# The mixture's first token group computed at the end of the scan's program, and the groups taken in the order 0, 2, 1, 3

## The chip, the core and the metric

The kernel runs on one NeuronCore of a Trainium2 chip. TensorE (PE in the profile, PEld for its weight loads), VectorE (DVE), ScalarE (ACT), GpSimd (POOL) and the sync engine (SP, which here only issues DMAs) each take their own list of instructions in order; semaphores order them against each other. The metric is the device time of one execution in microseconds (us), lower is better.

## What is computed

Two layers on x of shape 2 x 1024 x 256 in float32. Layer 0 is a causal linear attention and a feed-forward net with 2:4 sparsity. Layer 1 is a test-time-training scan and a mixture of experts; the change touches only these last two:

```python
x = x + ga * scan(layernorm(x) * (1 + ca) + sa)       # 64 minibatch steps of 16 tokens,
                                                      # out = layernorm(z) * gamma + beta, then @ Wo.T
h = layernorm(x) * (1 + cb) + sb
logits = h @ gate_w                                   # 8 experts, the best 2 by softmax
h1 = gelu(einsum('nd,edh->neh', h, w1) + b1)          # 8 experts of width 128
routed = einsum('ne,ned->nd', gates, einsum('neh,ehd->ned', h1, w2) + b2)
shared = gelu(h @ shared_w1 + shared_b1) @ shared_w2 + shared_b2
x = x + gb * (routed + shared)
```

## The kernel before, in words

Tokens lie in 16 tiles of 128 (x_sb): tiles 0 to 7 are batch row 0, tiles 8 to 15 batch row 1. The program has one block of instruction lists for each phase; a block ends with a barrier of all engines. The change touches the blocks of the last two phases.

**The scan** (scan_phase) walks eight chunks c; a chunk holds tile c of both batch rows and eight steps n. A step is values (L1628), residual on VectorE (L1428, u_done), gradient (L1640) and new_w on VectorE (L1433); other work, written out by hand, lies beside each step. The outputs z of a chunk go through DRAM or, for the last chunk, by small DMAs (L1223) to tokens on partitions; keep_z (L1270, GpSimd) makes z from them. Then follow, a chunk or two later, z_norm and z_aggregate (VectorE), z_rstd_of (GpSimd, L1275 and L1277), z_centre (VectorE, L1448), out_turn (TensorE, L1589), drain_out (ScalarE, L1363), the projection out_rows (TensorE, L1615), the gate out_rows (VectorE, L1455) and add_rows (GpSimd, L1290, x_done). In chunk 7 the normalised tiles 0 to 3 are turned (turn_group, L1730), drained (drain_group_norm, L1741), and split into a high part (L1413, hi_done) and a low part (GpSimd, L1330, hl_done): they are the mixture's group 0.

**The scan's tail**, after the last step, still has chunk 6's drain_out and out_rows and the whole chain of chunk 7. TensorE's list there is keep_warm(8), out_rows of chunk 6, out_turn(7), keep_warm(2), out_rows of chunk 7. keep_warm (L1659) multiplies the identity with a weight and nobody reads the result.

**The mixture** (moe_phase) takes four groups of four tiles, software-pipelined: the loop's turn g computes group g's outputs (shared_rows, expert_rows, weigh) beside group g+1's inner blocks. The first turn, g = -1, has only the latter: ten hidden(0, m) of six matmuls each (L1966), logits (L1949, sixteen matmuls), the turn of group 1 (L1730) and gates_turn (L1956). On ScalarE it has ten gelu activations (L1841) with bias, on VectorE memsets of gates (L1922), norms of group 1 (L204, L207), gating (L1868 to L1898), centring (L220) and split_group (L1749, L1751), on GpSimd two constants (L1807, L1808), an inverse root (L213) and ratio_of (L1813), which gating waits for in its middle. hidden(n) waits for the gelu two before it, since the PSUM tensor hid has two halves. The turn g = 0 begins with hidden(1, 0).

## Time and profile of the kernel before

| | us |
|---|---|
| median of three runs | 1066.62 |
| the three runs | 1066.62, 1066.68, 1062.79 |
| the profiled execution, its own time | 1061.99 |
| the profiled execution, its span | 1060.0 |

| engine | busy us | share of the span |
|---|---|---|
| PE | 995.6 | 94% |
| PEld | 800.8 | 76% |
| DVE | 678.6 | 64% |
| ACT | 332.5 | 31% |
| POOL | 250.2 | 24% |

The profile shows one execution. Durations are of one instruction or of a run of like instructions; PE's ends are modelled, so that for a series of matmuls the distance from one start to the next is the safer measure. "PE busy" counts every matmul, read or unread. The granted clock of TensorE is 0.986 of full speed in the mean; 1.00 is 2.4 GHz, 0.50 is 1.2 GHz.

### The profile page before, as it was taken

Reading aid. Unit: us, or ns where it says so; the run is one execution under the profiler, and the core shown is the slowest. Engines: PE = TensorE matmul, PEld = TensorE weight load, DVE = VectorE, ACT = ScalarE, POOL = GpSimd, SP = SyncE. Lnnn points to the kernel's source line nnn. Section 1 sums busy time; section 2 is a strip of 40 time slices with the busy share of each in tenths; the row PEclk is TensorE's granted clock in tenths of the full one; section 3 lists DMA queues with packets and bytes.
Section 4 is the critical chain, followed back from the end, with each engine's and each line's share of the span. In section 5 each row is a group of like instructions: output and inputs, shape, how many; then the busy total and the mean of one; then the engine's idle time right before and its main releaser. Section 6 shows DMA issues by size and latency. Waiting matters only on the chain. (4 is left out here: it accounts for less than half of the span.)

```text
span 1060.0 us, 15726 instructions
## 1 busy us (share of the span) xinstructions
PE 995.6 (94%) x6016; PEld 800.8 (76%) x6016; DVE 678.6 (64%) x1494; ACT 332.5 (31%) x604; POOL 250.2 (24%) x319
## 2 busy tenths in 40 slices
PE   6899999999999999999779999977999997999997
PEld 4688888888888888888668888864666664887875
DVE  6766676666676666666648887562667763466556
ACT  4343333343433333433224232102132421422220
POOL 2222222222221222222010100123344633111011
PEclk9999999999999999999999999998999999999999
DMA  9300000000000000000030000002544430000000
GB/s 293 134 2 1 1 1 1 1 1 2 1 1 1 1 1 1 2 1 1 20 124 10 1 1 1 1 1 44 139 128 97 87 72 7 1 16 16 11 21 20
DMA packets 33051, 33.37 MB, mean 31 GB/s; under 512 B 6857, under 2 KB 26834, under 8 KB 32978
## 3 DMA queue, kind: packets, MB, share of 16 engines
q1 hardware_dynamic: 32978, 32.38, 11.0%
q8 instruction: 48, 0.79, 0.3%
q14 instruction: 25, 0.20, 0.1%
HBM read 23.98 MB, written 8.13 MB: 30 GB/s over the span
## 5 line engine op out<-in xcount | busy, mean ns | idle before, releaser
L393 POOL TENSOR_TENSOR rope_sum<-rope_cos,rope_sin 128x512 f32<-128x512 f32 x80 | 114.9, 1436 | 257.2 <-DVE rope_sin L514 257.2
L429 ACT ACTIVATE rope_exp<-rope_sum 128x512 f32<-128x512 f32 x80 | 50.5, 631 | 205.5 <-POOL rope_sum L393 205.4
L783 PE MATMUL proj<-wo_sb,attn_out_t 128*128 128x256 f32 x512 | 113.2, 379 | 0.7 <-issue 0.7
L783 PEld LDWEIGHTS proj<-wo_sb,attn_out_t 128*128 128x128 f32 x512 | 96.1, 190 | 13.4 <-issue 0.9
L732 PE MATMUL num<-v_ones,score_masked 128*128 128x129 f32 x512 | 100.2, 278 | 5.9 <-DVE score_masked L572 5.9
L733 PE MATMUL num<-state,q_t 128*128 128x129 f32 x512 | 99.9, 277 | 0.0
L1910 DVE SCALAR_TENSOR_TENSOR m_acc<-m_expert,gates,m_acc 128x256 f32<-128x256 f32 x128 | 61.9, 484 | 49.0 <-PE m_expert L1991 42.2
L732 PEld LDWEIGHTS num<-v_ones,score_masked 128*128 128x128 f32 x512 | 83.0, 193 | 13.4 <-DVE score_masked L572 8.0
L511 DVE TENSOR_TENSOR rope_cos<-proj,cos_sb 128x512 f32<-128x512 f32 x80 | 55.3, 691 | 52.5 <-PE proj L686 52.5
L686 PE MATMUL proj<-w_hi,a_h_hi 128*128 128x512 f32 x192 | 79.4, 494 | 4.0 <-DVE w_lo L136 2.1
L733 PEld LDWEIGHTS num<-state,q_t 128*128 128x128 f32 x512 | 78.6, 194 | 0.0
L526 DVE SCALAR_TENSOR_TENSOR feat<-rope_sum,rope_exp 128x512 f32<-128x512 f32 x80 | 69.1, 864 | 6.9 <-ACT rope_exp L431 6.9
L724 PE MATMUL score<-q_t,k_t 128*128 128x512 f32 x128 | 66.9, 605 | 0.0
L1991 PE MATMUL m_expert<-w_sb,m_act 128*128 128x256 f32 x256 | 62.9, 385 | 3.3 <-DVE m_acc L1910 3.3
L1072 PE MATMUL f_rows<-wd_sb,hidden 128*128 128x256 f32 x256 | 58.1, 380 | 5.4 <-DVE f_dx L991 2.9
L1433 DVE TENSOR_TENSOR t_w<-g_ps,head_blocks 128x512 f32<-128x512 f32 x64 | 44.3, 691 | 29.0 <-PE g_ps L1640 28.9
L714 PEld LDWEIGHTS turn<-ident,feat 128*128 128x128 f32 x320 | 38.1, 142 | 32.3 <-issue 25.8
L686 PE MATMUL proj<-w_lo,a_h_hi 128*128 128x512 f32 x192 | 61.1, 399 | 0.0
L686 PE MATMUL proj<-w_hi,a_h_lo 128*128 128x512 f32 x192 | 61.0, 399 | 0.0
L1072 PEld LDWEIGHTS f_rows<-wd_sb,hidden 128*128 128x128 f32 x256 | 48.2, 190 | 13.9 <-issue 6.0
L1991 PEld LDWEIGHTS m_expert<-w_sb,m_act 128*128 128x128 f32 x256 | 47.3, 190 | 14.9 <-DVE m_acc L1910 8.8
L714 PE MATMUL turn<-ident,feat 128*128 128x128 f32 x320 | 46.4, 276 | 9.8 <-ACT k_t L416 9.8
(218 smaller groups left out, 1905.3 us busy)
## 6 DMA issues: line engine op xcount, KB each, us to landing
kv_scratch<-t_kv SPq DMA_DIRECT2D x16, 256.0 KB, 2.5
kv_rows<-kv_scratch SPq DMA_DIRECT2D x32, 128.0 KB, 3.5
a_stage<-in_wqkv SPq DMA_DIRECT2D x6, 512.0 KB, 5.5
wo_sb<-in_wo SPq DMA_DIRECT2D x1, 2048.0 KB, 9.4
a_stage<-in_wgu SPq DMA_DIRECT2D x4, 512.0 KB, 9.6
out<-x_sb SPq DMA_DIRECT2D x16, 128.0 KB, 1.7
u_scratch<-u_rows SPq DMA_DIRECT2D x28, 64.0 KB, 2.8
t_u<-u_scratch SPq DMA_DIRECT2D x14, 128.0 KB, 2.1
```

What stands on the lines that cost most here:

```text
L393: pool.tensor_tensor(y[:, parity], t1[:, parity], t2[:, parity], ALU.add).then_inc(s["y_done"], 1)
L511: dve.tensor_tensor(t1[:, parity].rearrange("p (g d) -> p g d", d=HD // 2), proj[:, bank, :].rearrange("p (g d) -> p g d", d=HD // 2), cc. ...
L526: dve.scalar_tensor_tensor(dst, y[:, parity], 0.0, ex[:, parity], ALU.max, ALU.add).then_inc(s["feat_done"], 1)
L686: mm = pe.matmul(proj[:, bank, :], hh[:, parity, k, :], ww[:, k, cols], start=(i == 0 and k == 0), stop=(i == 2 and k == KD - 1))
L714: t = pe.transpose(turn[:, bank(j), r * P:(r + 1) * P], src[:, r * P:(r + 1) * P], ident[:])
L724: pe.matmul(score[:, g % 2, :], k_t[:, g, :], q_t[:, g, :], start=True, stop=True).then_inc(s["score_full"], 1)
L732: pe.matmul(dst, am[:, g % 2, r * P:(r + 1) * P], v[:, b, g, :], start=True, stop=False)
L733: mm = pe.matmul(dst, q_t[:, g, r * P:(r + 1) * P], state[:, b, g, :], start=False, stop=True)
L783: mm = pe.matmul(proj[:, b, 0:D], o_t[:, i, :], wo[:, i, :], start=(i == 0), stop=(i == H - 1))
L1072: mm = pe.matmul(rows[:, n % 2, 0:D], hid[:, g % 2, m, i * P:(i + 1) * P], wd[:, m, :], start=(m == 0), stop=(m == NM - 1))
L1910: ins = dve.scalar_tensor_tensor(acc[:, n % 2], expert[:, k % 2, j * D:(j + 1) * D], gates[:, g % 2, i, e:e + 1], acc[:, n % 2], ALU.mult, ...
L1991: mm = pe.matmul(expert[:, k % 2, j * D:(j + 1) * D], act_t[:, g % 2, e, toks], w2[:, e, :], start=True, stop=True)
```

## The change

The mixture's turn g = -1 is taken out of moe_phase. Its instructions now stand in the scan's block, behind the last step, between those of chunks 6 and 7, and keep_warm(8) and keep_warm(2) are gone. The helpers gating, gates_turned, logits, gates_turn, ratio_of and hidden become methods with the same instructions; ScalarE's hidden is now called gelu. The PSUM tensors of the scan are used for them: kv_ps for hid, z_ps for small, g_ps for turn. The other part is the order of the groups: tiles 0 to 3, 8 to 11, 4 to 7, 12 to 15, so that the second group's tiles are those of chunks 0 to 3 of batch row 1. The memsets of gates go to the start of VectorE's list in the scan, GpSimd's constants to the end of its chunk 0, and the low part of group 0 moves forward in GpSimd's chunk 7, from its end to just before z_rstd_of. The three staging slots of the mixture's weights now lie in the tensor that the first group's gelu outputs are written to. In GpSimd's tail, z_rstd_of(7) now stands before add_rows(6).

The diff, cut to its core:

```diff
+TURNS = (0, 2, 1, 3)
...
-    def group_norm(self, s):
+    def group_norm(self, s, order=tuple(range(NG))):
...
-                dve.bn_stats(stats[:, i, :], x[:, g * GT + i, :]).then_inc(s["stat_done"], 1)
+                dve.bn_stats(stats[:, i, :], x[:, order[g] * GT + i, :]).then_inc(s["stat_done"], 1)
...
+        self.e_act = [self.keep.enter_context(nc.sbuf_tensor("m_act0", [P, NH, GT * P], F32))]
...
-            self.stage_for(ctx, "t_stage", NCH, 3)
+            self.first, self.slots = NCH, 3
+            self.stage = self.e_act[0][:].rearrange("p m t -> p (m t)")[:, 0:3 * KD * WCH].rearrange(
+                "p (s k n) -> p s k n", s=3, k=KD)
...
-            _, e_rstd, _ = self.group_norm(e_s)
+            e_norms, e_rstd, e_centre_group = self.group_norm(e_s, TURNS)
...
+                    if not nxt:
+                        pool.wait_ge(e_s["hi_done"], 1)
+                        pool.tensor_tensor(self.e_h_lo[:, 0], self.e_h[:], self.e_h_hi[:, 0].bitcast(F32), ALU.subtract
+                                           ).then_inc(e_s["hl_done"], 1)
                     if prev:
                         for b in range(B):
                             z_rstd_of(c - 1, b)
...
                     if c in (4, 5, 6):
                         i = c - 4
                         self.chunk_low(pool, NCH + i, i * WCH, min(WCH, NH * P - i * WCH))
-                    if not nxt:
-                        pool.wait_ge(e_s["hi_done"], 1)
-                        pool.tensor_tensor(self.e_h_lo[:, 0], self.e_h[:], self.e_h_hi[:, 0].bitcast(F32), ALU.subtract
-                                           ).then_inc(e_s["hl_done"], 1)
+                    if c == 0:
+                        self.gate_constants(pool)
+                e_rstd(pool, 1)
+                self.ratio_of(pool, 0)
                 for b in range(B):
                     keep_z(NC - 1, b)
                 for b in range(B):
+                    z_rstd_of(NC - 1, b)
+                for b in range(B):
                     add_rows(NC - 2, b)
-                for b in range(B):
-                    z_rstd_of(NC - 1, b)
                 for b in range(B):
                     add_rows(NC - 1, b)
...
-                for c in (NC - 2, NC - 1):
-                    for b in range(B):
-                        drain_out(c, b)
+                act.wait_ge(self.moe_in, 16 * 4)
+                self.gelu(act, 0, 0, kv_ps)
+                for b in range(B):
+                    drain_out(NC - 2, b)
+                for m in range(1, 4):
+                    self.gelu(act, 0, m, kv_ps)
+                self.gates_turned(act, 0, z_ps)
+                self.drain_group_norm(act, 1, g_ps)
+                self.gelu(act, 0, 4, kv_ps)
+                for b in range(B):
+                    drain_out(NC - 1, b)
+                for m in range(5, NH):
+                    self.gelu(act, 0, m, kv_ps)
...
+                self.clear_gates(dve)
...
+                dve.wait_ge(x_done, nth(1, GT))
+                e_norms(dve, 1)
+                self.gating(dve, 0, z_ps)
+                e_centre_group(dve, 1)
                 for b in range(B):
                     z_norm(NC - 1, b)
                 for b in range(B):
...
                     out_rows(NC - 2, b)
                 for b in range(B):
                     z_centre(NC - 1, b)
+                self.split_group(dve, 1)
                 for b in range(B):
                     out_rows(NC - 1, b)
...
-                pe.wait_ge(u_done, NC * NMB)
-                keep_warm(8)
-                for c in (NC - 2, NC - 1):
-                    if c == NC - 1:
-                        out_turn(c)
-                        keep_warm(2)
+                def last_rows(c):
                     for b in range(B):
                         for k in range(KD):
                             out_rows(c, b, k)
+                pe.wait_ge(self.moe_in, 16 * 4)
+                pe.wait_ge(self.w_ready, NCH + 3)
+                pe.wait_ge(e_s["hl_done"], 1)
+                self.hidden(pe, 0, 0, kv_ps)
+                pe.wait_ge(u_done, NC * NMB)
+                self.logits(pe, 0, z_ps)
+                self.hidden(pe, 0, 1, kv_ps)
+                last_rows(NC - 2)
+                for m in range(2, 4):
+                    self.hidden(pe, 0, m, kv_ps)
+                self.gates_turn(pe, 0, z_ps)
+                self.turn_group(pe, 1, g_ps)
+                self.hidden(pe, 0, 4, kv_ps)
+                out_turn(NC - 1)
+                self.hidden(pe, 0, 5, kv_ps)
+                last_rows(NC - 1)
+                for m in range(6, NH):
+                    self.hidden(pe, 0, m, kv_ps)
...
-        s, b = self.moe_s, g * GT // NC
+        s, b = self.moe_s, TURNS[g] * GT // NC
...
+    def gate_constants(self, pool):
+        lane, euler = self.e_gate["lane"], self.e_gate["euler"]
+        pool.iota(lane[:], pattern=[[1, E]], base=0, channel_multiplier=0, allow_small_or_imprecise_dtypes=True)
+        pool.memset(euler[:], float(np.e)).then_inc(self.moe_s["const_made"], 1)
+        pool.wait_ge(self.moe_s["const_made"], 1)
+    def clear_gates(self, dve):
+        s, gates = self.moe_s, self.e_gate["gates"]
+        dve.memset(gates[:], 0.0).then_inc(s["gate_step"], 1)
+        dve.wait_ge(s["gate_step"], 1)
+        dve.memset(gates[:, :, :, E:E + 1], 1.0)
+    def gating(self, dve, g, small):
...
+    def ratio_of(self, pool, g):
+        s, euler = self.moe_s, self.e_gate["euler"]
+        ratio, diff = self.e_gate["gate_ratio"], self.e_gate["logit_diff"]
+        pool.wait_ge(s["top_step"], 3 * g + 3)
+        pool.tensor_tensor(ratio[:], euler[:].broadcast_to([P, GT]), diff[:], ALU.pow).then_inc(s["ratio_done"], 1)
...
+    def gelu(self, act, g, m, hid):
+        s, b1, n = self.moe_s, self.moe_small[1], g * NH + m
+        act.wait_ge(s["hid_full"], n + 1)
+        act.activation(self.e_act[g % 2][:, m], hid[:, n % 2, :], ACT.Gelu, bias=b1[:, m:m + 1]
+                       ).then_inc(s["act_done"], 1)
...
+    def hidden(self, pe, g, m, hid):
+        s, n = self.moe_s, g * NH + m
+        w_hi, w_lo, h_hi, h_lo = self.w_hi, self.w_lo, self.e_h_hi, self.e_h_lo
+        if n >= 2:
+            pe.wait_ge(s["act_done"], n - 1)
...
+            def tile(n):
+                return TURNS[n // GT] * GT + n % GT
...
-                for g in range(-1, NG):
+                for g in range(NG):
                     if g + 2 < NG:
                         norms(dve, g + 2)
                     for i in range(GT):
-                        if g >= 0:
-                            for k in range(E // 2):
-                                weigh(g, i, k)
-                            gate_rows(g, i)
+                        for k in range(E // 2):
+                            weigh(g, i, k)
+                        gate_rows(g, i)
                         if i == 0 and g + 1 < NG:
-                            gating(g + 1)
+                            self.gating(dve, g + 1, small)
...
-                pe.wait_ge(self.moe_in, 16 * 4)
-                pe.wait_ge(self.w_ready, self.chunks + 3)
-                for g in range(-1, NG):
+                for g in range(NG):
                     if g + 1 < NG:
                         pe.wait_ge(s["hl_done"], g + 2)
                     for m in range(NH):
                         i, part = (m - 1) // 2, (m - 1) % 2
-                        if g >= 0 and 0 <= i < GT:
+                        if 0 <= i < GT:
                             if part == 0:
                                 shared_rows(g, i)
                             expert_rows(g, i, range(part * E // 4, (part + 1) * E // 4))
                         if g + 1 < NG:
-                            hidden(g + 1, m)
+                            self.hidden(pe, g + 1, m, hid)
                             if m == 0:
-                                logits(g + 1)
+                                self.logits(pe, g + 1, small)
...
-                        gates_turn(g + 1)
+                        self.gates_turn(pe, g + 1, small)
...
```

## Rows read from the trace of the kernel before

**Rows 1.** Chain that ended last, from 902 us: start, us, what.
```profile
903.95 1.68 PE m_small L1949 x16
...
912.60 0.87 PE m_turn L1730 x8
913.47 5.47 PE m_hid L1966 x24
```

**Rows 2.** Timeline, PE, 881 to 920: start, us, line, operation [idle before].
```profile
881.27 7.03 PE L1659 MATMUL z_ps<-t_wo,ident 128*128 128x512 f32 x16
888.14 1.89 PE L1615 MATMUL t_turn<-t_wo,t_o 128*128 128x256 f32 x8
894.11 1.05 PE L1589 MATMUL t_turn<-ident,t_zn 128*128 128x128 f32 x4 [4.08 <-DVE t_zn L1448]
...
898.01 1.89 PE L1615 MATMUL t_turn<-t_wo,t_o 128*128 128x256 f32 x8
902.34 0.70 PE L1966 MATMUL m_hid<-m_h_hi,w_hi 128*128 128x512 f32 x2 [2.44 <-PEq L1122]
...
918.78 0.60 PE L1956 MATMUL m_small<-ident,gates 128*128 128x128 f32 x4
919.14 0.71 PE L1966 MATMUL m_hid<-m_h_hi,w_hi 128*128 128x512 f32 x2
```

**Rows 3.** Windows: stretch, busy us by engine, PEclk, DMA share, GB/s.
```profile
734.00:735.00 1.00, 1.00 (x11) 0.61 (x10) 0.60 (x2) 0.00 (x0) 0.00 (x0) 0.50 0.00 0
...
895.00:896.00 1.00, 1.00 (x3) 0.48 (x3) 0.00 (x0) 0.81 (x3) 0.00 (x0) 0.50 0.00 0
...
901.00:902.00 1.00, 0.00 (x0) 0.00 (x0) 0.00 (x0) 0.00 (x0) 0.84 (x2) 1.00 0.00 0
```

**Rows 4.** Timeline, ACT, 881 to 915, columns as in rows 2.
```profile
881.25 1.50 ACT L1363 ACTIVATE t_o<-t_turn,ln_beta,ln_gamma 128x128 f32<-128x128 f32 x4 [10.13 <-PE t_turn L1589]
...
904.03 1.28 ACT L1841 ACT_TABLE_LOAD   x1 [7.33 <-PE m_hid L1966]
905.32 0.69 ACT L1841 ACTIVATE m_act<-m_hid,b_sb 128x512 f32<-128x512 f32 x1
...
913.22 1.44 ACT L1741 ACTIVATE m_h<-m_turn,mod_t 128x512 f32<-128x512 f32 x2
```

**Rows 5.** Timeline, DVE, 861 to 910, columns as in rows 2.
```profile
861.38 0.97 DVE L1448 TENSOR_SCALAR t_zn<-t_z,t_mv,t_rstd 128x256 f32<-128x256 f32 x1
...
888.43 0.43 DVE L1438 BATCH_NORM_STATS2 t_stats<-t_z 128x6 f32<-128x256 f32 x1 [0.81 <-POOL t_z L1270]
888.77 0.30 DVE L1442 BATCH_NORM_AGGREGATE t_mv<-t_stats 128x2 f32<-128x6 f32 x2
890.06 0.76 DVE L1455 TENSOR_TENSOR t_dx<-t_turn,gate_b 128x256 f32<-128x256 f32 x2 [0.99 <-PE t_turn L1615]
...
893.64 0.41 DVE L1448 TENSOR_SCALAR t_zn<-t_z,t_mv,t_rstd 128x256 f32<-128x256 f32 x1 [0.45 <-POOL t_rstd L1277]
...
902.44 0.91 DVE L1922 MEMSET gates<- 128x1024 f32 x1 [1.75 <-PEq L1122]
...
905.67 0.19 DVE L1868 COPY logits_sb<-m_small 128x32 f32<-128x32 f32 x1 [0.60 <-PE m_small L1949]
...
909.29 0.19 DVE L1897 TENSOR_TENSOR gates<-picked 128x32 f32<-128x32 f32 x1
```

**Rows 6.** Timeline, POOL, 713 to 902, columns as in rows 2.
```profile
713.43 3.51 POOL L1256 MEMSET kv_rows<- 128x4096 f32 x1 [0.31 <-POOLq L809]
...
861.48 1.46 POOL L1290 TENSOR_TENSOR x_sb<-x_sb,t_dx 128x256 f32<-128x256 f32 x2
...
880.31 2.40 POOL L1330 TENSOR_TENSOR m_h_lo<-m_h,m_h_hi 128x1024 fp32r<-128x1024 f32 x1
...
887.67 0.72 POOL L1270 TENSOR_TENSOR t_z<-t_kv,t_u 128x256 f32<-128x256 f32 x1 [0.52 <-DMA t_u<-u_rows]
...
900.44 1.40 POOL L1290 TENSOR_TENSOR x_sb<-x_sb,t_dx 128x256 f32<-128x256 f32 x2 [6.84 <-DVE t_dx L1455]
```

More of the change, by code:

```diff
@@ L45 @@
 E, EH = 8, 128
+NH = E + 2
 GT = 4
 NG = NT // GT
+TURNS = (0, 2, 1, 3)
 WCH = 512
@@ L1121, in scan_phase @@
             ("w2_sb", [P, NH, D]), ("b1_sb", [P, NH]), ("b2_sb", [P, D]), ("gate_w_sb", [P, KD, E]))]
+        self.e_act = [self.keep.enter_context(nc.sbuf_tensor("m_act0", [P, NH, GT * P], F32))]
+        self.e_gate = {n: self.keep.enter_context(nc.sbuf_tensor(n, shape, dt)) for n, shape, dt in (
+            ("logits_sb", [P, GT, E], F32), ("top", [P, GT, E], F32), ("top_at", [P, GT, E], U32),
+            ("top_at_f", [P, GT, 2], F32), ("lane", [P, E], F32), ("euler", [P, 1], F32), ("logit_diff", [P, GT], F32),
+            ("gate_ratio", [P, GT], F32), ("gate_total", [P, GT], F32), ("gate_pair", [P, 2, GT], F32),
+            ("picked", [P, 2, GT, E], F32), ("gates", [P, 2, GT, P], F32), ("gates_t", [P, 2, GT, P], F32))}
         with ExitStack() as ctx:
@@ new lines, in gelu, with logits @@
+    def gelu(self, act, g, m, hid):
[3 more added lines that the diff above has]
+                       ).then_inc(s["act_done"], 1)
+    def logits(self, pe, g, small):
+        s, h, gw = self.moe_s, self.e_h, self.moe_small[3]
+        pe.wait_ge(s["h_done"], KD * (g + 1))
+        if g:
+            pe.wait_ge(s["gturn_done"], g)
+        for i in range(GT):
+            for k in range(KD):
+                mm = pe.matmul(small[:, i * E:(i + 1) * E], h[:, k, i * P:(i + 1) * P], gw[:, k, :],
+                               start=(k == 0), stop=(k == KD - 1))
+        mm.then_inc(s["logit_full"], 1)
@@ new lines, in gates_turn @@
+    def gates_turn(self, pe, g, small):
+        s, gates = self.moe_s, self.e_gate["gates"]
+        pe.wait_ge(s["gates_done"], g + 1)
+        for i in range(GT):
+            t = pe.transpose(small[:, i * P:(i + 1) * P], gates[:, g % 2, i, :], self.ident[:])
+        t.then_inc(s["gturn_full"], 1)
+    def hidden(self, pe, g, m, hid):
[3 more added lines that the diff above has]
+            pe.wait_ge(s["act_done"], n - 1)
+        cols = slice(m * P, (m + 1) * P)
+        for i, (ww, hh) in enumerate([(w_hi, h_hi), (w_lo, h_hi), (w_hi, h_lo)]):
+            for k in range(KD):
+                mm = pe.matmul(hid[:, n % 2, :], ww[:, k, cols], hh[:, g % 2, k, :],
+                               start=(i == 0 and k == 0), stop=(i == 2 and k == KD - 1))
+        mm.then_inc(s["hid_full"], 1)
```

164 lines of the change are left out of this document (58 added, 106 removed).

## The prediction

> **What bounds the kernel now.** I read the chain of work that ended last first. From the mixture's first instruction on it is TensorE almost without a break: six matmuls of a hidden block after six, logits, the turn [rows 1]. Then I read TensorE's timeline over the scan's tail and the first turn [rows 2]. The reader is to see three kinds of time in it. From 881.27 to 888.14 sixteen records of keep_warm (eight float32 products of two passes), and from about 894.95 to 898.01 four more (two products): 6.9 and 3.1 us in which TensorE is called busy and computes nothing that is read. Then two idle times, 4.08 us before out_turn(7) and 2.44 us before the first hidden block. Last, real work: two times eight matmuls of out_rows, one out_turn, and from 902.34 to 919.14 the whole turn g = -1, 16.80 us. The other engines' timelines show that they are nearly empty there: ScalarE has two drain_out of 1.50 us and was idle for 10.13 us before the first [rows 4]; VectorE and GpSimd wait for z and for each other [rows 5, 6]. So the tail is a chain of latencies (last residual, DMAs, z at 888.39, statistics, root, centring, turn, drain, projection, add), and the first turn a stretch of TensorE work, and now they stand one behind the other. The change lays the second into the first.
>
> **What the tail costs when TensorE has it all.** Per step: a hidden block is 5.47 / 4 = 1.37 us, say 1.39 behind other work; logits 1.68; the turn of group 1 0.87 [rows 1]; gates_turn 919.14 - 918.78 = 0.36; eight matmuls of out_rows 1.89 by their modelled ends, 1.75 as distance to what follows; out_turn about 0.5 at full clock (the 1.05 of its row lies in a slow stretch) [rows 2]. Ten hidden blocks 13.8, and 1.68 + 0.87 + 0.36 + 3.5 + 0.5: 20.7 us. From 881.27 that would end at 902.0 without any wait.
>
> **The waits, in the order of TensorE's new list.** Three waits stand ahead of it, and all of the tail is queued behind them. The weights and the DMAs are long in. The low part of group 0, which took GpSimd from 880.31 to 882.71 [rows 6], now comes before z_rstd_of(6); its high part was ready at 881.25 - 10.13 = 871.1 [rows 4], so it runs in the free time ahead of chunk 6's statistics and ends before 881. Cover gone, this wait would cost at most 1.4 us. Nothing is late.
>
> hidden(0,0) ends at 882.7. ScalarE's first gelu stands before drain_out(6), with the table load ahead of it: 1.28 + 0.69 [rows 4], so 884.75, then the drain, 886.25. Before, the drain ended at 882.75, but there its user waited for keep_warm until 888.14. TensorE meanwhile does logits (884.4) and hidden(0,1) (885.8), waits 0.5 us, and does out_rows(6) from 886.3 to 888.0.
>
> A page bears on the load. The Trainium skill, "ScalarE: Activation LUTs", section "What ACT_TABLE_LOAD costs", gives 1.28 us and a drain of 1.38 us with it. The row shows the load right behind the matmul's end and the gelu 1.29 us later, so here the drain does not appear on an engine that had been idle; by the page's total the drain_out(6) would end 1.4 us later and so would everything, a forecast 1.4 us higher.
>
> Then hidden(0,2) and (0,3) to 890.8, gates_turn to 891.15, the turn of group 1 to 892.0, hidden(0,4) to 893.4. gates_turn needs VectorE's gating: from logits, 905.67 to 909.48 or 3.8 us [rows 5], of which one piece is GpSimd's ratio_of; from 884.5 that is 888.3. It has 2.5 us to spare. VectorE's norms of group 1 fit between its last residual at 880.1 and the logits. GpSimd waits in ratio_of until 885.9 and is free at 886.9; z(7,1) started at 887.67 behind its DMA [rows 6], which doesn't move, as SP's list is unchanged.
>
> The chain of chunk 7 is later than before at its start: behind gating VectorE centres group 1 (four of about 0.35, 889.7), where before the statistics began with the second z at 888.43. Then two statistics to 890.4, two aggregates (0.30) to 890.7, two products (0.76) to 891.5 [rows 5]. The roots no longer stand behind add_rows(6) on GpSimd, which in the before cost them 1.4 us: they are ready at 891.6 and 892.4 (two operations each, 0.75 together), and the second t_zn at 892.8, where it ended at 894.05 before [rows 5]. But add_rows(6) now starts in that very moment. At 861.38 a t_zn beside GpSimd's x_sb add took 0.97 instead of 0.41 [rows 5, 6], so I take 893.3. The Trainium skill, "SBUF — State Buffer", section "Who interferes with whom", has the port shared by the two as locked for a whole instruction; by that t_zn may wait for one add of 0.7 us or two, and the second alone would make the sum 0.6 us longer. TensorE is at 893.4: out_turn(7) goes on time, to 893.9, hidden(0,5) to 895.3.
>
> ScalarE does gelu 2 and 3, gates_t (0.6), the drain of group 1 (1.44) [rows 4] to 893.5, gelu 4, and drain_out(7) to about 895.7. TensorE waits 0.45 us; out_rows(7) to 897.5. Before, these began at 898.01, behind the second keep_warm at half clock. Four hidden blocks are left: 903.0. ScalarE's last gelu 0.75 after: 903.75. GpSimd's last add (before 901.84 [rows 6]) would be ready near 899.6 and is no longer the end; split_group (about 2 us of VectorE) fits before the product of chunk 7's rows. The barrier took 902.34 - 901.84 = 0.5 us [rows 2, 6]. So hidden(1,0) begins at 904.25 and not at 919.14 [rows 2]: **14.9 us**. From there the list is that of before; in the old turn g = 0 the first products of VectorE waited for TensorE, and norms of the third group (1.8 us) now start with the block and are over before them.
>
> **What is added elsewhere.** The memset of gates (0.91 [rows 5]) stands at the head of the scan's VectorE list. Statistics behind it are 1 us later, but GpSimd, their user, is then in its own memset of 3.51 us from 713.43 [rows 6]: hidden. If the two memsets hinder each other, that memset is on the path and it costs up to 0.9; no row shows them together, the add beside t_zn is the nearest and there one of them paid 0.6; I take 0.2 and keep 0 to 0.9. The two constants (a quarter of a us) fall where GpSimd waits. The order of the groups costs nothing: the same tiles, the same DMAs, the last group the same. No gain is left for the end of the kernel. Sum: 14.9 - 0.2 = **14.7 us**.
>
> **To the number.** Against the profiled execution, 1061.99, this is 1047.3. The median of the runs is 1066.62, and the four executions shown lie in two pairs, near 1062.4 and near 1066.6. The gain is the same in either; the median of the changed kernel may fall at 1047.5 or at 1052. I take 1051, with more weight on the level of the median. Ends: without the waits of about 1 us and nothing for the memset, 16.1 us saved; with a drain (1.4), the lock (0.6), the memset (0.9) and 1 us of unseen slips, 11. From the two levels that is 1046 to 1056, and I give 1045.5 to 1056.5.
>
> **Rivals.**
>
> Chain late (0.12). The centring of chunk 7 comes to stand last, because VectorE does gating and centring of group 1 first. For it: it uses up 5.2 us between logits and statistics, and TensorE keeps its order, so each us after 893.4 is a us lost. Against it: roots come earlier than before. If the second t_zn ends at 896, out_turn and all that follows are 2.6 us later: 1053.6.
>
> Clock (0.07). The unread matmuls filled TensorE until the chain's next link. In the trace the granted clock fell to 0.50, 1.2 GHz, after the idle 4.08 us and again near 734 after an idle stretch in the scan's first chunk; it was 1.00 through the 2.44 us before the mixture [rows 2, 3]. The new list has gaps of half a us and 1.25 us at the barrier. One fall of some 6 us, as at 734, costs about 3: 1054.
>
> Clock, the other side (0.03). The same mechanism held: if the clock falls at the first gap, 885.8, and does not return through the tail, the remaining 16 us of its work take 32, and 5 us of the first mixture turn's work take 5 more: 21 lost against 14.7 won, 1057 to 1073 by where it returns; it is slower than before from some 15 us of TensorE work at 1.2 GHz on. I name 1072. Against it: the falls seen ended within 7 us of work.
>
> Given back (0.06). The change does not do what it says: the turn moves, but the mixture's later turns are paced by something that doesn't start sooner. For it, VectorE's products take part in the chain of the later turns. Against it, everything they need comes from TensorE, and nothing in that block is tied to a clock outside. It would give 1062 to 1066.
>
> The forecast itself has 0.72. Within 0.5% (5.3 us, about what a measurement of this kernel tells from no change) is 0.06, slower 0.03, faster by more than 0.5% the rest, 0.91.
>
> **What would show it.** In the new profile: no row of a warm matmul after the last step; hidden(0,0) within 0.2 us of the last out_turn's neighbour near 881.3; the table load in the tail; gates about 888.3; second t_zn near 893; out_rows(7) from about 895.7; the barrier near 904 and the first hidden(1, .) of the mixture's block near 904.3; a clock of 1.00 throughout; the mixture's block (old turn g = 0 to the end) as long as the 141 us of before. A gap of more than 1 us before out_turn(7) proves the first rival, a PEclk under 1.00 in the tail the second, a longer mixture block the last. The prediction is wrong if out_turn's chain is over 3 us late or the start of the scan has moved by more than 1 us.

## The result, and the profile after

| | us |
|---|---|
| kernel before, median of 4 runs (1060.33 to 1066.68) | 1064.7 |
| changed kernel, median of 4 runs (1046.39 to 1049.88) | 1049.31 |
| ratio, 95% interval | 0.9849 [0.9815, 0.9882] |
| changed kernel, the profiled execution and its span | 1049.88, 1047.9 |

The kernel is faster by 1.5%: the interval lies wholly under 1, and 1.5% of 1064.7 us is 16.1 us, with an interval from 12.6 to 19.7. A later repetition gave 0.9865 [0.9813, 0.9917] with a median of 1047.95 (six runs). Runs over 1.5% above the fastest of their kernel stand in the medians but are left out of the ratios, so a ratio can differ a little from the quotient of two medians.

To see where the time went I cut the span of each profiled execution at three points that all kernels have: the scan's first instruction on TensorE, its last u_rows on VectorE, and the first m_shared matmul of the mixture's turn g = 0.

| stretch, us | before | after | difference |
|---|---|---|---|
| start to the scan's start (same code) | 713.47 | 715.27 | +1.80 |
| the scan's steps | 166.38 | 166.99 | +0.61 |
| **tail and first turn** | 42.47 | 28.25 | **-14.22** |
| first m_shared to the end | 137.68 | 137.39 | -0.29 |

The whole gain is in the third line. The first line is code that the change doesn't touch. It is longer since the granted clock was lower in the attention, 0.91 in the mean over the first 60 us against 0.97 before; at 60 us the changed kernel is 1.81 us behind, which is the whole of it. One stretch of each, from the windows of the kernel before and then of the kernel after (columns as in rows 3):

```profile
25.00:30.00 5.00, 4.95 (x23) 4.27 (x23) 5.00 (x6) 1.85 (x3) 1.65 (x1) 1.00 1.10 348
```

```profile
25.00:30.00 5.00, 5.00 (x16) 4.01 (x16) 5.00 (x7) 1.50 (x3) 1.71 (x2) 0.66 1.10 348
```

With the clock at 0.66 TensorE got 16 matmuls done where it had done 23. (PEclk is the column before the last two.)

TensorE's timeline of the changed kernel through the tail (start, us, line, operation, idle before it), to be read beside rows 2:

```profile
882.96 0.66 PE L1619 MATMUL t_turn<-ident,t_zn 128*128 128x128 f32 x4 [0.35 <-DVE t_zn L1472]
883.46 0.39 PE L1700 MATMUL z_ps<-head_blocks,ident 128*128 128x128 f32 x2
883.60 0.70 PE L1901 MATMUL kv_ps<-m_h_hi,w_hi 128*128 128x512 f32 x2
...
885.07 1.85 PE L1880 MATMUL z_ps<-gate_w_sb,m_h 128*128 128x8 f32 x16
...
888.74 1.99 PE L1645 MATMUL t_turn<-t_wo,t_o 128*128 128x256 f32 x8 [0.36 <-ACT t_o L1377]
...
893.31 0.60 PE L1889 MATMUL z_ps<-ident,gates 128*128 128x128 f32 x4
893.74 1.04 PE L1774 MATMUL g_ps<-ident,g_xn 128*128 128x128 f32 x8
...
896.43 0.66 PE L1619 MATMUL t_turn<-ident,t_zn 128*128 128x128 f32 x4 [0.26 <-DVE t_zn L1472]
...
898.68 1.99 PE L1645 MATMUL t_turn<-t_wo,t_o 128*128 128x256 f32 x8 [0.20 <-ACT t_o L1377]
...
901.90 0.62 PE L1901 MATMUL kv_ps<-m_h_hi,w_hi 128*128 128x512 f32 x2
...
903.28 0.61 PE L1901 MATMUL kv_ps<-m_h_hi,w_hi 128*128 128x512 f32 x2
...
904.64 0.61 PE L1901 MATMUL kv_ps<-m_h_hi,w_hi 128*128 128x512 f32 x2
...
907.34 0.70 PE L1901 MATMUL m_hid<-m_h_hi,w_hi 128*128 128x512 f32 x2 [1.18 <-PEq L1130]
...
910.51 0.68 PE L2033 MATMUL m_shared<-b_sb,gates_t 128*128 128x256 f32 x2
```

No unread matmul is left. Where TensorE had been idle for 4.08 and 2.44 us [rows 2] it now waits 0.36, 0.26 and 0.20 us inside the tail and 1.18 us at the barrier. hidden(0,0) starts at 883.60, in the place of keep_warm at 881.27 [rows 2], and the block's hidden(1,0) is at 907.34, 23.74 us behind it; before, the same distance was 919.14 - 881.27 = 37.87. The clock held through all of it, as the windows of the changed kernel show:

```profile
880.00:890.00 10.00, 9.29 (x70) 7.48 (x67) 5.93 (x33) 3.94 (x7) 5.22 (x9) 1.00 0.07 13
890.00:900.00 10.00, 9.54 (x50) 7.58 (x49) 8.08 (x21) 5.98 (x11) 4.11 (x8) 1.00 0.01 2
900.00:906.00 6.00, 6.00 (x28) 4.76 (x26) 0.76 (x2) 2.06 (x3) 1.44 (x2) 1.00 0.00 0
```

### The profile page after: what moved, and what is told of

Its sections match the earlier page's. It is cut to its first block and busy times, and to the rows that moved or that the text cites. A ratio compares the mean times of both kernels' runs of the same rounds, so it can differ in the third digit from the quotient of the medians.

```text
span 1047.9 us, 15691 instructions
## 1 busy us (share of the span) xinstructions
PE 987.6 (94%) x5996; PEld 797.3 (76%) x5996; DVE 678.9 (65%) x1494; ACT 332.2 (32%) x604; POOL 250.6 (24%) x319
## 5 line engine op out<-in xcount | busy, mean ns | idle before, releaser
L2047 PEld LDWEIGHTS m_expert<-w_sb,m_act 128*128 128x128 f32 x256 | 47.3, 190 | 14.5 <-DVE m_acc L1998 8.5
```

The lines of the kernel that those rows point to most:

```text
L2047: mm = pe.matmul(expert[:, k % 2, j * D:(j + 1) * D], act_t[g % 2][:, e, toks], w2[:, e, :], start=True, stop=True)
```

## The experiments

The theory is that of the prediction: real work now fills the time of the unread products and of the chain's waits, and the tail is as long as its work on TensorE with waits of about a us. The rivals: the order of the groups or the moved constants bring something; leaving the unread products out is by itself the gain (or the loss, through the clock); the chain of chunk 7 is the true bound. "Tail" below is the stretch from the last u_rows to the first m_shared, in one profiled execution of each kernel. In brackets behind a median stands the ratio to the kernel before on the same chip, with its 95% interval. The kernels ran on several chips, so compare the ratios rather than the medians.

| kernel | median, ratio | tail of the profiled execution |
|---|---|---|
| before | 1064.7 | 42.47 |
| before, unread products left out | 1068.08 (1.0007 [0.9963, 1.0052]) | 48.74 |
| before, order alone | 1064.75 (0.9979 [0.9942, 1.0015]) | 45.28 |
| after | 1049.31 (0.9849 [0.9815, 0.9882]) | 28.25 |
| after, unread products put back | 1057.21 (0.9907 [0.9846, 0.9968]) | 36.24 |
| after, parts one behind the other | 1060.2 (0.996 [0.9933, 0.9987]) | 39.39 |
| after, chain 2.2 us later | 1051.26 (0.9854 [0.9758, 0.995]) | 31.42 |
| after, chain 4.4 us later | 1055.52 (0.9894 [0.9794, 0.9993]) | 33.68 |
| after, 7 unread at the scan's start | 1053.51 (0.9867 [0.9805, 0.9929]) | 28.45 |
| after, 2 and 8 unread there | 1054.26 (0.9899 [0.9856, 0.9941]) | 28.2 |
| after again | 1047.95 (0.9865 [0.9813, 0.9917]) | 28.22 |
| after, tail reordered | 1047.96 (0.9856 [0.9818, 0.9894]) | 27.99 |

**The unread products alone.** From the kernel before, nothing else changed:

```diff
-                keep_warm(8)
                 for c in (NC - 2, NC - 1):
                     if c == NC - 1:
                         out_turn(c)
-                        keep_warm(2)
```

> The kernel before without keep_warm(8) and keep_warm(2), nothing else. Theory A (the gain is the mixture's turn laid over the tail; the unread products only fill): chunk 7's chain still sets the tail, second t_zn at the same distance from the last residual, so hidden(1,0) of the mixture comes no more than about 1 us sooner (out_rows(7) no longer waits for the second keep_warm) or, with the slower clock it may leave, up to 2 us later: time within 0.3% of before. Theory B (most of the gain is simply the ten unread products gone, 9.9 us of TensorE): about 8 to 10 us faster than before. Clock rival: the granted clock falls to 0.50 in the idle 4 to 9 us and part of the mixture's first turn runs at 1.2 GHz, 2 to 4 us slower than before.

Measured: no gain, and in the profiled execution a tail of 48.74 us, 6.3 longer, which is more than any of the three forecasts had. TensorE's timeline of this kernel, and its windows:

```profile
883.91 1.97 PE L1615 MATMUL t_turn<-t_wo,t_o 128*128 128x256 f32 x8 [1.47 <-ACT t_o L1363]
895.08 1.11 PE L1589 MATMUL t_turn<-ident,t_zn 128*128 128x128 f32 x4 [9.21 <-DVE t_zn L1448]
897.79 3.78 PE L1615 MATMUL t_turn<-t_wo,t_o 128*128 128x256 f32 x8 [1.60 <-ACT t_o L1363]
904.02 1.19 PE L1964 MATMUL m_hid<-m_h_hi,w_hi 128*128 128x512 f32 x2 [2.44 <-PEq L1122]
...
926.41 0.71 PE L1964 MATMUL m_hid<-m_h_hi,w_hi 128*128 128x512 f32 x2
```

```profile
889.00:890.00 1.00, 0.00 (x0) 0.00 (x0) 0.43 (x1) 0.00 (x0) 0.49 (x2) 0.50 0.04 8
...
902.00:904.00 2.00, 0.00 (x0) 0.01 (x1) 0.37 (x2) 0.00 (x0) 1.55 (x4) 0.50 0.00 0
...
905.00:906.00 1.00, 1.00 (x4) 0.80 (x3) 0.95 (x5) 0.00 (x0) 0.00 (x0) 0.50 0.00 0
915.00:916.00 1.00, 1.00 (x4) 0.81 (x3) 0.28 (x1) 0.51 (x1) 0.00 (x0) 0.50 0.00 0
916.00:917.00 1.00, 1.00 (x5) 0.76 (x5) 0.00 (x0) 0.17 (x1) 0.00 (x0) 0.97 0.00 0
```

TensorE stands idle for 9.21 us, the clock is at 1.2 GHz from about 889 to 916, and the mixture's first turn takes 926.41 - 904.02 = 22.4 us instead of 16.8 [rows 2]. So in this execution the unread products were not waste: without them the tail is 6.3 us longer. The runs don't show as much: the ratio of 1.0007 is 0.7 us, and its interval goes from 3.9 us faster to 5.5 us slower. What holds for both is that leaving the products out gains nothing. The chain of chunk 7 was as long with them as without (its second t_zn starts 13.77 us behind the last u_rows, 13.79 before), and what could be gained was the time of real work laid into it, not their removal. The clock rival of the prediction has a real price; it did not come due in the tail of the changed kernel, where the clock stayed at 1.00 and no idle time is over 1.2 us.

**The order alone.** From the kernel before, with the groups in the order 0, 2, 1, 3 (the same lines as in the change; the turn and the memsets stay in the mixture). The moved constants had no run of their own; what the profiles show of them stands further below.

> The kernel before with only the order of the groups changed to 0, 2, 1, 3. Theory A and B: no change, within 0.3% of before, the mixture's block as long as before to 0.3 us. Only a rival that credits the order itself (other tiles free sooner, another pattern of output DMAs) expects more than 3 us either way.

Measured: no change, as expected; the interval holds 1. In the profiled execution the clock was at 0.50 over 735 to 752 in the scan, which makes its stretch of steps 171.35 instead of 166.38. Its tail is 45.28 us and not 42.47, though it holds the same instructions with the same idle times of 4.08 and 2.44 us. The difference is the clock, which in the kernel before was low in the tail only from about 894.2 to 897.6:

```profile
902.00:905.00 3.00, 3.00 (x6) 1.66 (x5) 0.00 (x0) 0.16 (x1) 0.00 (x0) 0.50 0.00 0
...
908.00:911.00 3.00, 2.00 (x5) 1.65 (x6) 1.86 (x5) 0.00 (x0) 0.67 (x3) 0.65 0.00 0
```

So the old tail varies by some 3 us with the clock alone, and its 42.47 us is a good one. The order is there only to have the second group's tiles ready.

**The unread products put back into the changed kernel.**

```diff
+                def unread(times):
+                    for _ in range(times):
+                        pe.matmul(g_ps[:, 3, :], ident[:], ...)
+                pe.wait_ge(u_done, NC * NMB)
+                unread(8)
                 pe.wait_ge(self.moe_in, 16 * 4)
...
                 out_turn(NC - 1)
+                unread(2)
```

> The changed kernel with the unread products put back: eight ahead of hidden(0,0), two behind out_turn(7), into a bank nobody uses. If TensorE's list sets the tail of the changed kernel, as the sum said, they cost nearly their whole length there: 6.9 + 1.7 us less the 0.8 us in which it waited, so about 7.8 us longer than the changed kernel and still some 6.5 us (0.6%) under before. If the chain of chunk 7 sets it, at most 2 us longer than the changed kernel.

Measured: the tail is 36.24 - 28.25 = 7.99 us longer; 7.8 was expected. TensorE has next to no slack there: the ten products take 6.46 and 1.32 us from their start to that of what follows, and the waits of 0.26 and 0.20 us all but go (the one of 0.36 stays, at 0.34). In part the agreement is luck: the products are shorter than the 8.6 us reckoned with, and they cover less than the 0.8 us of waits.

**The same work without the lapping.** The changed kernel, but each engine first does chunks 6 and 7 and then the mixture's first turn, in the scan's block:

```diff
 (ScalarE)
-                self.gelu(act, 0, 0, kv_ps)
-                for b in range(B):
-                    drain_out(NC - 2, b)
-                for m in range(1, 4):
+                for c in (NC - 2, NC - 1):
+                    for b in range(B):
+                        drain_out(c, b)
+                for m in range(6):
                     self.gelu(act, 0, m, kv_ps)
...
 (TensorE)
                 pe.wait_ge(u_done, NC * NMB)
                 last_rows(NC - 2)
                 out_turn(NC - 1)
                 last_rows(NC - 1)
+                self.hidden(pe, 0, 0, kv_ps)
+                self.logits(pe, 0, z_ps)
+                for m in range(1, 6):
+                    self.hidden(pe, 0, m, kv_ps)
...
```

> The changed kernel with the same instructions in the same block, but the mixture's turn wholly behind chunk 7's out_rows on every engine, without unread products. Theory A: the whole latency chain is bare again; second t_zn about 1 us sooner than before (roots ahead of add_rows(6)), then out_rows(7) at about 895.5 on the scale of before, the turn's 16.8 us, gates_turn, ScalarE and the barrier: hidden(1,0) some 2 to 4 us sooner than before, so 10 to 12 us slower than the changed kernel; 2 us more if the clock falls in the idle time. Theory B (it is the unread products, or the block boundary, not the overlap): within 3 us of the changed kernel.

Measured: 11.14 us more than the changed kernel and 3.1 less than before, both inside what was expected. The ratios agree: 0.996 here, 0.9849 and 0.9865 for the changed kernel, with intervals that don't meet. TensorE waits as in the first experiment:

```profile
893.82 1.12 PE L1616 MATMUL t_turn<-ident,t_zn 128*128 128x128 f32 x4 [7.00 <-DVE t_zn L1469]
896.53 3.46 PE L1642 MATMUL t_turn<-t_wo,t_o 128*128 128x256 f32 x8 [1.60 <-ACT t_o L1377]
```

```profile
890.00:899.00 9.00, 3.59 (x10) 2.72 (x11) 2.51 (x7) 2.79 (x5) 3.57 (x7) 0.50 0.00 0
```

Of the 14.2 us, then, 11.1 come with the lapping, in the same block and with the same instructions. Some 1.5 of them are clock: out_rows(7) takes 3.11 us here (896.53 to 899.64) and 1.65 in the changed kernel. The share also depends on what else is in the kernel: with the unread products in both, the tail goes from 42.47 to 36.24, by 6.2 us.

The other 3.1 come with the rest of the change. Beside the timeline of before [rows 2], out_turn(7) comes 2.2 us sooner behind the last u_rows (12.07 against 14.26), out_rows(7) another 1.2 sooner behind it, with no keep_warm(2) between, hidden(0,0) another 1.2, with no barrier between, and from there to hidden(1,0) it is 1.55 longer (18.35 against 16.80), with the barrier in it. For the 2.2 us of the chain the candidates are the root of chunk 7 ahead of add_rows(6) and the low part of group 0 ahead of it. I did not take these apart, and the tail of before alone varies by nearly as much.

**The chain of chunk 7 made later.** The changed kernel with a memset of an unused stretch behind e_centre_group on VectorE (one, then two):

```diff
                 e_centre_group(dve, 1)
+                dve.memset(kv_r[:, 0, 0:8], 0.0)
```

> The changed kernel with one memset of 2048 columns (about 1.8 us of VectorE, into a buffer that is dead by then) behind the centring of group 1, ahead of z_norm(7). In the changed kernel TensorE waited 0.26 us for the second t_zn, so the chain of chunk 7 and TensorE's list were level there. If the first rival's price holds (each us behind that point is a us lost), the stretch from the last u_rows to the first m_shared grows from 28.25 us by 1.7 to 1.9 us. If TensorE's list alone set the tail, by under 0.5 us.

```diff
                 e_centre_group(dve, 1)
+                dve.memset(kv_r[:, 0], 0.0)
+                dve.memset(kv_r[:, 1, 0:8], 0.0)
```

> The same with 6144 columns of memset, about 5.4 us, which opens an idle stretch of some 5.5 us ahead of out_turn(7). Chain alone: the stretch from the last u_rows to the first m_shared is 5.4 us longer than in the changed kernel, 33.7 us. With the clock rival's mechanism: the granted clock falls to 0.50 in or behind that idle stretch, as it did after the idle 4.08 us of the kernel before and the 9.21 us of e1_before_no_unread, and the work behind it costs 2 to 5 us more: 36 to 39 us.

One line of TensorE's timeline of each, and a window of the first:

```profile
898.04 1.11 PE L1620 MATMUL t_turn<-ident,t_zn 128*128 128x128 f32 x4 [2.48 <-DVE t_zn L1472]
```

```profile
897.41 1.12 PE L1621 MATMUL t_turn<-ident,t_zn 128*128 128x128 f32 x4 [4.61 <-DVE t_zn L1472]
```

```profile
899.00:901.00 2.00, 2.00 (x6) 1.60 (x6) 1.35 (x2) 1.51 (x4) 0.00 (x0) 0.50 0.00 0
```

The idle time before out_turn(7) grew from 0.26 to 2.48 and 4.61 us, by 2.2 and 4.35; the tail by 3.17 and 5.43. So in these two profiles each us of the chain is a us of the tail, and about one more is the clock, which stands at 0.50 or 0.56 for two us or more behind either gap: from out_turn(7) to hidden(1,0) it is 11.81 and 11.96 us instead of 10.91. The chain is on the path, then, and the "chain late" rival was the right thing to fear: it lies 0.26 us behind TensorE's work. The medians are of two runs each and can't tell 3 us apart.

Neither forecast had the sum right. For the smaller delay I had expected 1.7 to 1.9 us and no clock. For the larger one the chain alone was to give 33.7 us and the clock 36 to 39; 33.68 looks like the chain alone, but that is chance. I had reckoned with 6144 columns and 5.4 us, and kv_r[:, 0] has 2048, as many as kv_r[:, 1, 0:8]: the timeline has two memsets of 1.76 us. The delay was 4.4 us, and a us of clock made up the rest, not 2 to 5.

**The scan's start.** Both kernels lose time there to the clock: in the changed kernel TensorE is busy without a break at 735 to 740 and the granted clock is 0.58. Window of the changed kernel:

```profile
735.00:740.00 5.00, 5.00 (x32) 3.16 (x33) 2.41 (x8) 0.00 (x0) 1.45 (x4) 0.58 0.00 0
```

Two kernels try to buy it back with more unread products ahead of the first step:

```diff
-                keep_warm(4)
+                keep_warm(7)
```

> The changed kernel with keep_warm(7) in place of keep_warm(4) at the start of the scan: three more unread products, 2.6 us at full clock, in an idle time of 2.89 us ahead of the first gradient that a DMA ends. In all profiles so far the granted clock is 0.50 for 6 to 15 us behind that idle time. If the fall comes of the idle time, the scan's first steps run at 1.00 and the kernel is 2.5 to 8 us faster than the changed one, with less spread, so 0.9765 to 0.982 of before; if the clock falls anyway, no change or up to 2 us slower by the products at half clock (0.985 to 0.987 of before).

```diff
                 for b in range(B):
                     ...project(0, b, i)
+                pe.wait_ge(self.small_in, 16 * 5)
+                keep_warm(2)
...
-                keep_warm(4)
+                keep_warm(8)
```

> The changed kernel with two unread products ahead of the first k_turn, in an idle time of 2.2 us, and eight in place of four behind it. If both idle times cost the clock there, the eight products run at full clock (7 us) and the first steps too: as fast as e7_scan_start_7 or up to 1 us faster. If the clock is at 0.50 when they begin, they take up to 13 us, outlast the DMA by 3 to 6 us, and this is slower than e7_scan_start_7 by as much.

The first window of the first of them, what came later in it on TensorE and VectorE, and the window of that:

```profile
735.00:740.00 5.00, 5.00 (x57) 3.17 (x55) 3.74 (x10) 0.39 (x2) 1.13 (x2) 1.00 0.15 56
```

```profile
788.84 0.50 PE L1670 MATMUL g_ps<-u_rows,kv_rows 16*128 16x128 f32 x8 [2.33 <-DVE u_rows L1452]
```

```profile
788.49 0.29 DVE L1452 TENSOR_TENSOR u_rows<-kv_rows,z_ps 128x128 f32<-128x128 f32 x1 [3.13 <-DMA kv_rows<-kv_scratch]
```

```profile
790.00:800.00 10.00, 10.00 (x64) 5.71 (x63) 4.20 (x13) 0.39 (x1) 3.55 (x7) 0.54 0.16 54
```

Chunk 0, from its first u_rows to the next chunk's, took 17.8 us in both instead of 20.75, as expected: the mechanism works where it is applied. But 1.8 us are lost again by the end of chunk 2, and in both: it takes 20.70 and 20.71 us instead of 18.91, as VectorE waits 3.13 us in either for a kv_rows load where the changed kernel waits 1.33. Counted from the first u_rows, chunk 2 starts 2.4 and 2.7 us sooner than in the changed kernel, but that load is issued only 0.5 and 0.8 us sooner; why is open. And in chunk 3 of the one and in chunk 5 of the other (25.43 us each, about 18.4 otherwise) the clock fell again, in the first right behind that load, in the second behind an idle time of 1.21 us. The scan's steps took 173.57 and 174.55 us instead of 166.99. The gain of 2.5 to 8 us that I expected of the first did not come: the medians are about 4 and 5 us above the changed kernel's of 1049.31, the ratios (0.9867 and 0.9899 against 0.9849 and 0.9865) have intervals that overlap its own. Whether the extra products make the later fall likelier, or whether each of the two profiled executions happened on one, is open; the result gives no reason to keep them.

**A repetition and a reordered tail.** Against the waits of 0.36, 0.26 and 0.20 us, ScalarE's drain_out(6) goes ahead of the first gelu, its drain of group 1 behind drain_out(7), VectorE's centring of group 1 behind the statistics of chunk 7, and TensorE's list follows:

```diff
                 act.wait_ge(self.moe_in, 16 * 4)
-                self.gelu(act, 0, 0, kv_ps)
                 for b in range(B):
                     drain_out(NC - 2, b)
-                for m in range(1, 4):
+                for m in range(4):
                     self.gelu(act, 0, m, kv_ps)
...
-                e_centre_group(dve, 1)
                 for b in range(B):
...
                     z_aggregate(NC - 1, b)
+                e_centre_group(dve, 1)
```

> The changed kernel once more, nothing changed, for a second profile and more runs. The account so far: the stretch from the last u_rows to the first m_shared is 28.25 us in every profile of it (to 0.3 us), the stretch behind it 137.4, and what varies from run to run is where the granted clock falls to 0.50 ahead of the tail, in the attention's first 40 us and in the scan. So 0.982 to 0.989 of before, and the times of its runs order themselves by their mean clock. If the tail varied instead, its stretch would differ by more than 1 us.

> The changed kernel with three pieces moved in its tail: drain_out(6) ahead of the first gelu and its table load, with out_rows(6) ahead of hidden(0,1); z_norm and z_aggregate of chunk 7 ahead of the centring of group 1; the turn of group 1 and its drain behind hidden(0,4) and drain_out(7). This takes TensorE's waits of 0.36 and 0.26 us away, if they came from the table load ahead of drain_out(6) and from gating and centring ahead of the statistics. Stretch from the last u_rows to the first m_shared 27.5 to 27.8 us in place of 28.25; the time, by 0.6 us, can't be told from e9_after_again. If TensorE's list doesn't set the stretch, it stays at 28.2 or grows.

```profile
894.11 0.66 PE L1618 MATMUL t_turn<-ident,t_zn 128*128 128x128 f32 x4 [0.59 <-DVE t_zn L1471]
```

The line is TensorE's, of the reordered kernel. The wait for drain_out(6) is gone, but the one before out_turn(7) is 0.59 us instead of 0.26: TensorE came 0.6 us sooner and the chain only 0.26 (13.91 us behind the last u_rows, 14.17 in the changed kernel). The tail is 27.99 us against 28.22, where 27.5 to 27.8 was expected, and the median 1047.96 against 1047.95. It is no version worth having over the changed kernel.

## Why the prediction was right

It named 1051.0 within 1045.5 to 1056.5, by a gain of 14.7 us; the stretch that the change touches got 14.2 us shorter and the median is 1049.31. The 14.2 us are what bears the mechanism out. That the median fell within 1.7 us of 1051.0 is in part luck: by the medians the gain is 15.4 us, by the two profiled executions 12.1, as the clock differs outside the tail, and in the old tail too from execution to execution (42.47 and 45.28 us). Point by point, counted from the instruction behind the last out_turn of the steps (881.27 before [rows 2], 883.60 after):

| | forecast | measured | row of after |
|---|---|---|---|
| out_rows(6) starts | 5.0 | 5.14 | 888.74 |
| gating over | 7.0 | 8.05 | 891.65 |
| statistics of chunk 7 start | 8.4 | 9.34 | 892.94 |
| second t_zn ends | 12.0 | 12.78 | 896.38 |
| out_turn(7) starts | 12.1 | 12.83 | 896.43 |
| out_rows(7) starts | 14.5 | 15.08 | 898.68 |
| hidden(1,0) of the block | 23.0 | 23.74 | 907.34 |

**The order of events held; two terms were mis-sized.** drain_out(6) behind the table load, the wait of 0.45 us before out_rows(7) (0.20) and the barrier (1.18 us of idle TensorE; 1.25 forecast) came out within 0.3 us each. By 0.7 us at out_turn(7) and 0.8 at the end the tail is later than forecast, and it is so on two sides at once.

The first is the work on TensorE. From 883.60 to the last product's end at 906.16 (907.34 less the wait of 1.18) it is 22.56 us; less the three waits, 0.82, that leaves 21.7 us of work, where I had 20.7. The six other pieces make 6.6 us (6.9 forecast); the ten hidden blocks make 15.1 and not 13.8. I took 1.39 us for each, from a stretch in which they stand back to back. Such a block takes 1.38 us here too (901.90 to 903.28, and 1.36 to 904.64), but one that starts behind another kind of product, or is followed by one or by a wait, takes 1.47 to 1.64 us (883.60 to 885.07; 896.84 to the wait that ends at 898.68, 1.64). Cut into pieces the turn has more such seams.

The second is gating: 3.8 us forecast, 4.6 measured (887.02 to 891.65). VectorE's timeline in the changed kernel and GpSimd's beside it:

```profile
887.02 0.19 DVE L1819 COPY logits_sb<-z_ps 128x32 f32<-128x32 f32 x1 [2.52 <-PE z_ps L1880]
...
889.90 0.53 DVE L1837 TENSOR_TENSOR gate_pair<-gate_ratio,gate_pair 128x4 f32<-128x4 f32 x1
...
891.00 0.72 DVE L1848 TENSOR_TENSOR gates<-picked 128x32 f32<-128x32 f32 x1
...
895.56 0.82 DVE L1472 TENSOR_SCALAR t_zn<-t_z,t_mv,t_rstd 128x256 f32<-128x256 f32 x1 [0.45 <-POOL t_rstd L1287]
```

```profile
889.69 0.72 POOL L1280 TENSOR_TENSOR t_z<-t_kv,t_u 128x256 f32<-128x256 f32 x1 [0.24 <-DMA t_u<-u_rows]
890.93 0.73 POOL L1280 TENSOR_TENSOR t_z<-t_kv,t_u 128x256 f32<-128x256 f32 x1 [0.52 <-DMA t_u<-u_rows]
...
895.50 1.47 POOL L1300 TENSOR_TENSOR x_sb<-x_sb,t_dx 128x256 f32<-128x256 f32 x2
```

The last gates operation took 0.19 us when GpSimd was idle [rows 5] and takes 0.72 here; it starts at 891.00 and is over when GpSimd's add, begun at 890.93, is. The one at 889.90 takes 0.53 in the same way. I had priced this lock for t_zn alone (0.97 against 0.41 us; it took 0.82) and had written "it has 2.5 us to spare" of gating, which is true of TensorE's gates_turn but not of chunk 7's statistics, queued behind it on VectorE. It makes the chain 0.8 us later: right mechanism, one instance missed. Which operation meets the add changes, the sum hardly does: in the repetition's profile the last gates operation took 0.19 us, and an earlier pair and the centring were longer instead (they took 0.29 and 1.05 us in the first profile); the statistics of chunk 7 began 10.63 us behind the last u_rows there and 10.68 here.

```profile
888.23 0.71 DVE L1844 TENSOR_TENSOR picked<-picked,gate_pair 128x32 f32<-128x32 f32 x2
...
889.41 1.48 DVE L223 TENSOR_SCALAR g_xn<-x_sb,g_mv,g_rstd 128x256 f32<-128x256 f32 x3
```

A reading behind it was wrong as well: z(7,1), 6.4 us behind the reference point before, "doesn't move", but it began after 7.3 us here (890.93), as its DMAs came later. It is not what the statistics waited for, since centring ended behind it, but it put the add beside the gates operation. Of the two, TensorE's own work was over at 896.17 and the chain at 896.38, so mending the chain alone would have brought out_turn(7) forward by 0.26 us at most, and mending TensorE's part ahead of it alone by nothing. By the Trainium skill, "SBUF — State Buffer", section "Who interferes with whom", an operation of VectorE with two inputs in SBUF contends with a GpSimd instruction that reads SBUF. The trace agrees, down to operations on 128x4 and 128x32 that took 0.53 and 0.72 us.

**The drain of the table load didn't come.** ScalarE's timeline in the changed kernel:

```profile
885.31 1.28 ACT L1869 ACT_TABLE_LOAD   x1 [11.79 <-PE kv_ps L1901]
886.60 0.69 ACT L1869 ACTIVATE m_act<-kv_ps,b_sb 128x512 f32<-128x512 f32 x1
887.19 1.50 ACT L1377 ACTIVATE t_o<-t_turn,ln_beta,ln_gamma 128x128 f32<-128x128 f32 x4
```

The gelu follows the load after 1.29 us. The 1.38 us of drain that the Trainium skill ("ScalarE: Activation LUTs", "What ACT_TABLE_LOAD costs") adds to it are not to be seen behind 11.79 us of idle ScalarE; it would have made out_rows(6) 1.4 us later, and that is 0.1 us late.

**The two memsets did not hinder each other.** I took 0.2 us within 0 to 0.9. VectorE's memset ran under GpSimd's, which took 3.52 us where it took 3.51 alone [rows 6]:

```profile
715.51 0.91 DVE L1808 MEMSET gates<- 128x1024 f32 x1 [1.40 <-PEq L812]
```

```profile
715.23 3.52 POOL L1266 MEMSET kv_rows<- 128x4096 f32 x1 [0.31 <-POOLq L812]
```

Still, the first u_rows comes 0.2 us later: 19.31 to 19.46 us behind the scan's start in the seven profiles with the change and the old start of the scan, 19.14 to 19.19 in the three profiles of kernels without it. That fits the 0.2 us, but whether the memset or another part of the change causes it is not shown.

**Nothing was given back.** From the first m_shared to the end it is 137.39 us against 137.68. The rival that the later turns are paced by something else is out.

**The base.** The forecast against the profiled execution was 1047.3; that execution took 1049.88. Of the 2.6 us between them +1.80 + 0.61 arose ahead of the tail, and 0.2 from there on (14.22 + 0.29 us won, 14.7 forecast). I had left room for it as two levels of the runs (1062.4 and 1066.6) without knowing what they are. They are not two levels: over 53 runs of the kernel before that were taken beside the experiments the time goes from 1060.7 to 1078.7 and follows the mean granted clock of the run, with a correlation of -0.99 and 0.89 us for each 0.001 of it; without the four longest it goes to 1076.8, with -0.99 and 0.90. My condition "wrong if the start of the scan moves by more than 1 us" was met (+1.80) without the change having a part in it: it should have been put on stretches with the clock at 1.00. One sum of the range is off too: without the waits of 0.5 and 0.45 us the gain would be 15.9 us and not 16.1.

**The rivals.** "Chain late" stood at 0.12 with 2.6 us: the chain was late by 0.8. "Clock" did not happen, though the profile of the first experiment shows what it can cost (6 us) and the delayed chain that an idle time of 2.48 us before out_turn(7) was enough for about 1 us. The ground I gave, that the clock was 1.00 through the 2.44 us of idle before the mixture [rows 2, 3], was weak: the same idle time of 2.44 us in the first experiment lies at 0.50 (902 to 904), where the clock had been since 889: in both cases what the clock was in the gap had been set ahead of it.

## What to carry to other kernels

Unread matmuls that hold TensorE's clock over a latency chain mark a place where real work of a later stage could stand; taking them away gained nothing by itself here (ratio 1.0007) and made the tail of the profiled execution 6.3 us longer. What the exchange gains is the length of the moved work plus the waits that it covers, provided every engine's list is laid in the order in which the chain's links come due: here the chain came out level with the work, within 0.26 us, so price each operation queued ahead of its links, the small ones of VectorE beside GpSimd too. Before a forecast is put against a median, see how much of the spread between runs is the clock.

## What the runs showed of the hardware

- **A busy TensorE at half clock.** In the kernel with the order alone the granted clock was 0.50 from 735 to 752 with TensorE busy for all 17.00 us, at the small products of the scan's steps; in chunk 5 of the kernel with 2 and 8 unread products 0.50 from 830 to 846 with 16.00 of 16 us busy. In the first experiment it stayed at 0.50 through the mixture's products too, from their start at 904 to 916, while behind the gaps of the delayed chain it was back after some 3 us. What decides how long it lasts no run here shows; the busy time of TensorE alone doesn't tell it. The windows of the first two:

```profile
735.00:752.00 17.00, 17.00 (x111) 11.14 (x104) 6.33 (x17) 1.15 (x3) 2.90 (x6) 0.50 0.25 65
```

```profile
830.00:846.00 16.00, 16.00 (x88) 9.36 (x88) 6.43 (x17) 0.77 (x2) 4.56 (x9) 0.50 0.24 66
```

- **The spread between runs is the clock.** Six runs of the changed kernel in its repetition: 1045.34 us at a mean clock of 0.990, 1047.01 at 0.990, 1047.74 at 0.988, 1048.15 at 0.987, 1049.36 at 0.985, 1060.88 at 0.974. In the profiled executions it falls in different places of the same code: the attention, and the scan's chunk 0, 3 or 5.
- **A memset of VectorE did not hinder one of GpSimd** (3.52 against 3.51 us), while operations of VectorE with two SBUF inputs were longer beside GpSimd's add: 0.53 us for one of 128x4 that took 0.16 before, 0.72 for one of 128x32 that took 0.19.
